# First layer's heads: the two query projections behind the smallest pair of query tiles

## What is computed

```
x = L0_attn_x
xn = _layernorm(x, axis=-1)
x = x + _L0_attn_ref(xn, w_q, w_kv, w_dense) + _L0_ffn_ref(xn, ...)
...
def _L0_attn_ref(x, w_q, w_kv, w_dense):
    q = jnp.einsum('bsh,he->bse', x, w_q).reshape(b, sq, GROUPS, HPG, KVC)
    k, v = jnp.split(jnp.einsum('bsh,he->bse', x, w_kv), 2, axis=-1)
    scores = jnp.einsum('bqgpd,bkgd->bgqpk', q, k) * SCALE
    scores = jnp.where(causal[None, None, :, None, :], scores, -jnp.inf)
    probs = jax.nn.softmax(scores, axis=-1)
    ctx = jnp.einsum('bgqpk,bkgd->bqgpd', probs, v).reshape(b, sq, HEADS * KVC)
    return jnp.einsum('bse,eh->bsh', ctx, w_dense)
```

## Time and profile before

| | us |
|---|---|
| three runs | 3680.51, 3680.76, 3674.75 (median 3680.51) |
| the profiled execution's own time | 3672.85 |
| its span | 3671.1 |
| PE busy in the span | 3376.9 (92%) |
| DVE, ACT, POOL busy | 2423.2, 1566.8, 1182.8 |
| the 16 heads of layer 0, in the span | 75 to 897 |

### The profile page before, as it was taken

The page is one execution under the profiler, slowest core; times in us unless marked ns, Lnnn a source line. Parts: engine busy times, 40 slices in busy tenths (PEclk is TensorE's granted clock), DMA queues, the critical chain, the costliest instruction groups (busy, mean ns, idle before and its releaser), DMA issues. The chain is left out here.

```text
span 3671.1 us, 65160 instructions
## 1 busy us (share of the span) xinstructions
PE 3376.9 (92%) x21360; PEld 2608.3 (71%) x21360; DVE 2423.2 (66%) x4492; ACT 1566.8 (43%) x2872; POOL 1182.8 (32%) x854
## 2 busy tenths in 40 slices
PE   8999999999979999999986779999779998799997
PEld 6888888887758788888862445555358886488883
DVE  4666666666335666566555778886478887488873
ACT  4555555554324444444432236666233333233332
POOL 4011010200236666666643200000124445344444
PEclk9999999999999999999998879999879999899998
DMA  5000000010001000000001412221144442244331
GB/s 176 4 18 11 7 20 3 26 37 1 0 7 50 18 19 13 19 16 19 17 0 53 154 70 81 81 81 61 61 113 113 111 112 68 58 118 110 108 98 49
DMA packets 134113, 199.98 MB, mean 54 GB/s; under 512 B 23120, under 2 KB 78288, under 8 KB 133968
## 3 DMA queue, kind: packets, MB, share of 16 engines
q1 hardware_dynamic: 127888, 190.55, 16.7%
q0 software_dynamic: 6144, 8.39, 1.4%
HBM read 162.06 MB, written 36.57 MB: 54 GB/s over the span
## 5 line engine op out<-in xcount | busy, mean ns | idle before, releaser
L2137 DVE TENSOR_REDUCE l2h_half<-l2h_s 128x1 f32<-128x512 f32 x512 | 337.2, 685 | 48.0 <-PE l2h_s L2039 45.4
L2124 ACT ACTIVATE l2h_PT<-l2h_s 128x1024 f32<-128x1024 f32 x256 | 248.4, 1023 | 163.5 <-PE l2h_s L2049 163.4
L791 DVE TENSOR_REDUCE l0h_negtop<-l0h_sc 128x1 f32<-128x128 f32 (+7 forms) x256 | 192.7, 753 | 161.9 <-PE l0h_sc L687 161.9
L813 DVE TENSOR_TENSOR l0h_PTL<-l0h_tp,l0h_PTH 128x512 fp32r<-128x512 f32 (+3 forms) x384 | 199.9, 549 | 135.3 <-ACT l0h_PTH L869 135.2
L869 ACT ACTIVATE l0h_PTH<-l0h_tp 128x512 fp32r<-128x512 f32 (+3 forms) x384 | 174.6, 490 | 199.5 <-PE l0h_tp L698 197.7
L2039 PE MATMUL l2h_s<-l2h_K,l2h_Q 128*128 128x512 f32 x512 | 219.1, 466 | 22.7 <-DMA l2h_K<-l_split 20.0
L879 ACT ACTIVATE l0h_probs<-l0h_sc,l0h_negtop 128x128 f32<-128x128 f32 (+7 forms) x256 | 191.1, 746 | 90.0 <-DVE l0h_negtop L791 86.3
L159 POOL TENSOR_TENSOR XN<-XN,n_rstd 128x512 f32<-128x512 f32 x24 | 29.9, 1267 | 566.5 <-DVE n_rstd L140 566.5
L765 POOL TENSOR_TENSOR l0a_wq_lo<-l0a_wq,l0a_wq_hi 128x256 fp32r<-128x256 f32 x15 | 11.1, 741 | 591.2 <-ACT l0a_wq_hi L853 591.2
L698 PE MATMUL l0h_tp<-ident,l0h_probs 128*128 128x128 f32 x1152 | 175.6, 277 | 21.4 <-DVE l0h_PTL L813 21.4
L713 PE MATMUL l0h_cx<-l0h_PTH,l0a_VH 128*128 128x256 f32 (+1 forms) x640 | 183.1, 286 | 0.7 <-DVE l0h_PTL L813 0.7
(11 more groups left out here) (449 smaller groups left out, 9903.9 us busy)
## 6 DMA issues: line engine op xcount, KB each, us to landing
l3p_decb<-l_decays SPq DMA_DIRECT2D x128, 256.0 KB, 4.4
l3p_w<-L_w SPq DMA_DIRECT2D x34, 512.0 KB, 3.7
l2h_Q<-l_split SPq DMA_DIRECT2D x64, 256.0 KB
l2h_K<-l_split SPq DMA_DIRECT2D x64, 256.0 KB
l3p_prow<-l_decays SPq DMA_DIRECT2D x128, 128.0 KB, 3.1
l_split<-l2q_hi SPq DMA_DIRECT2D x16, 512.0 KB, 3.6
l_split<-l2q_lo SPq DMA_DIRECT2D x16, 512.0 KB, 3.8
l3p_wgu<-L_ffn_w_gate_up SPq DMA_DIRECT2D x32, 256.0 KB, 4.8
```

Source lines behind the costliest of these rows:

```text
L791: dve.reduce_max(negtop[:, i % 4:i % 4 + 1], sc[s % 2][:, 0:(t + 1) * P], AX_X, negate=True).then_inc(top_ready, 1)
L813: dve.tensor_tensor(PTL[part], tp[n % 2][:, 0:m * P].rearrange("p (m n) -> p m n", m=m), PTH[part].bitcast(F32), ALU.subtract).then_inc(pt ...
L2124: act.activation(PT[:, b, kb, :], s2[kb % 2][:, :], ACT.Exp, scale=L2_SCALE).then_inc(exped, 1)
L2137: dve.reduce_max(half[:, b, t, z:z + 1], bank(slot_of(i))[:, :], AX_X).then_inc(s1_read, 1)
```

## The change

```
-    SLOTS = [("unit", i) for i in range(4)] + [("query", 1)] + [("unit", i) for i in range(4, 12)] + [("query", 0)] + [("unit", i) for i in range(12, 16)]
+    SLOTS = [("unit", i) for i in range(2)] + [("query", 1)] + [("unit", i) for i in range(2, 10)] + [("query", 0)] + [("unit", i) for i in range(10, 16)]
```

## The result

| | before | changed |
|---|---|---|
| median of 7 runs each | 3676.00 | **3659.13** |
| lowest and highest | 3669.98, 3683.11 | 3652.44, 3661.14 |
| profiled execution's own time, its span | 3672.85, 3671.1 | 3659.13, 3657.3 |

The ratio is 0.994, with a 95% interval of 0.9926 to 0.9955: faster by 16 to 27 us. The two medians differ by 16.9. The forecast was 3660, the range 3645 to 3672.

The account below looks back on a forecast made before the run. PE's stream was taken to bound the heads; about 0.6 us won per half over 32 halves, 19 to 20 us, gave 3672.85 - 20 = 3653 for the profiled execution and 3680.5 - 20 = 3660 as median, range 3645 to 3672.

Parts of the forecast that it names:

- The bound: In the 16 heads PE's stream sets the time, 51.4 us per head; only PE's 24.1 us of idle can be won.
- The place of the gain: At a half's start, weighing begins 1.25 us after the first score matmul instead of 1.94, the dense product standing between.
- The chain from tile 7's transposes: At the end of a half, from tile 7's transposes to the second PTL's end: 2.59 us; weighing starts 0.15 later.
- the forecast 50.2: PE's distance from one head to the next falls from 51.4 to about 50.2 us.
- The new wait: Amid tile 6's transposes PE waits 0.35 us for tile 3's PTL, behind tile 7's row maximum on DVE.
- the rest of the half: Up to the next half's start nothing is gained: about 273.0 against 272.93, wait won and wait made nearly cancelling.
- The room for DVE's additions: Moved additions stand ahead of tile 0's row maximum; its probabilities are first needed 6.5 us after the half's start.
- The waits that had to hold: Covers in each half: ctxT with 0.15 us left, POOL's low weights 3.6 us; projection readers finish before tile 3's scores.
- third rival: Dense product behind tile 6's scores waits for ctxT behind tile 3's exponential; at 0.9 us, 10 us slower, 3690; 5%.
- listed under "wrong": Signs of failure: head distance 51 us or more with a tile 6 or ctxT wait, or tile 3's scores awaiting queries' low part.
- The start's clock: At the first head's start, PE at 1.2 GHz: difference put at nothing, at most 2 us.
- The later layers keep their durations: Listed as a sign that the forecast is right: layers after the changed one take as long as before.

Follow-up runs that it names:

- first: Kernel before with its old slots, only the dense product of tiles 2 and 3 and its additions one step later: 3659.02 us against 3680.32, ratio 0.9945.
- third: Changed kernel with only batch 1's projection moved (slot 2), batch 0's left at slot 13: 3664.75 us, one run; 50.40 us per head.
- fourth: Changed kernel with the dense product of tiles 0 and 1 one step later, behind tile 3's transposes: 3644.70 us against 3680.32 before, ratio 0.9907.
- last of the experiments: Changed slots, late dense product of tiles 0 and 1, ACT and DVE doing queries ahead of tile 0's PTH and PTL: 3642.40 us, ratio 0.9904 to before.

## Why the prediction was right, and where its terms were off

**The bound** held. PE's stream sets the heads' time, and what was won is what PE waited.

**The place of the gain** was named rightly: the dense product between tile 7's transposes and tile 0's scores. The first and third experiments show it. The prediction put 0.69 us there (1.94 to 1.25) and the trace has 0.78 (1.94 to 1.16). The chain from tile 7's transposes to the second `PTL`'s end took 2.56 us (243.28 to 245.84), as reckoned (2.59). But the first score matmul came 1.56 us behind the start of those transposes, where 1.5 was put, and the weighing 0.16 behind `PTL`. The distance of the heads fell to 49.6 us, not only to the forecast 50.2.

**The new wait** was named with its place and its cause, and sized 0.35 us; it is 0.25. Together with small differences in the switches, the rest of the half gained 0.02 us instead of losing 0.07. That is the term that was mis-sized: 0.09 at the half's start and 0.09 in the rest make 0.80 instead of 0.62 us per half, 5 to 6 us over 32 halves.

**The room for DVE's additions** was put at 6.5 us from the half's start to the first need of tile 0's probabilities. That left out the projection, which now stands ahead of tile 0's transpose: in the changed kernel it is 8.8 us (244.84 to 253.61). The error was on the safe side.

**The waits that had to hold** did. `ctxT` for tiles 0 and 1 was ready at 235.53 (235.16 + 0.37) and its dense product started at 235.92:

```profile
235.16 0.37 ACT L887 ACTIVATE l0h_ctxT<-l0h_cx 128x256 f32<-128x256 f32 x1
...
235.92 1.03 PE L727 MATMUL l0h_outp<-l0a_wd,l0h_ctxT 128*128 x4
```

0.39 us were left, not 0.15. That the third rival was near is no mere thought: one slot further it made the kernel slower.

**Missed:** the first head. The prediction said that the readers of the projection finish before tile 3's scores need the bank, and priced only the steady heads. In the first half of head 0 no older pair is weighed between the projection and those scores, so the cover of 2.15 us isn't there (timeline of the changed kernel):

```profile
82.33 1.29 DVE L797 SCALAR_TENSOR_TENSOR l0a_QL<-l0h_sc,l0a_QH 128x512 fp32r<-128x512 f32 x2 [0.20 <-ACT l0a_QH L858]
...
83.67 0.50 PE L683 MATMUL l0h_sc<-l0a_KH,l0a_QH 128*128 128x512 f32 x1 [1.36 <-DVE l0a_QL L797]
```

It costs 1.36 us once, and is the wait that the prediction listed under "wrong".

**The start's clock** was put at no difference, and in this pair there is none: over 76 to 80 us the granted clock is 0.57 in both kernels, that is most of it at 1.2 GHz. The changed kernel (the clock is third from the end):

```profile
76.00:80.00 4.00, 3.60 (x13) 2.80 (x12) 0.71 (x2) 1.66 (x5) 3.19 (x1) 0.57 0.77 259
```

PE was a little busier in it (3.60 us instead of 3.45), and the slow stretch was no shorter. By the rule of the Trainium skill (TensorE: Matmul & The Clock Gate, Part 1) that recent activity releases the clock, up to 2 us more were thinkable; this pair shows none of it. But the slow start is not there in every execution. Over the same 4 us the clock is 1.00 in the first, third, fourth and last of the experiments, with PE busy 3.21 to 3.48 us, and 0.56 to 0.63 in the other four, with PE busy 3.45 to 4.00 us. So the higher clock goes neither with one order of the slots nor with a busier PE in these 4 us, and what decides it stays open. It is worth over 1 us: the first projection takes 4.06 us to the next start in the change, and 2.91 in the fourth experiment, whose order is the same there.

**"The later layers keep their durations"** was wrong for this pair of profiles, and why is only known in part. POOL splits the weights of layer 1 in 17 steps, the last 16 of them one per head; first and last start, before and after:

```profile
L1372 POOL TENSOR_TENSOR l1a_w_lo<-l1a_w,l1a_w_hi x17: 1802/1813/1821, 1101.0 to 1876.3; 128x768 fp32r<-128x768 f32 x17
```

```profile
L1372 POOL TENSOR_TENSOR l1a_w_lo<-l1a_w,l1a_w_hi x17: 1800/1814/1820, 1079.6 to 1859.7; 128x768 fp32r<-128x768 f32 x17
```

775.3 us from first to last before, 780.1 after. The change doesn't touch this layer, and the eight experiments, most of which change the first layer's heads as much, have 775.1 to 777.4. That speaks for a property of the execution and not of the change; with one profile of the changed kernel it isn't shown.

With this the profiled pair can be followed from start to end, by how far the changed kernel is ahead of the one before. Where the first layer's second part starts it is 22.9 us (903.76 against 880.89, next section): 22.4 from the 14 distances, less 1.4 up to the first head's split (95.9 to 97.3), where the 1.36 us lie, and 1.8 won behind the last split. At the first split of layer 1 it is 21.4, after the clock's 1.7 (next section); at its last 16.6; at POOL's first split of layer 3 16.9 and at the last 13.7 (its 34 splits took 866.6 us before and 869.8 after, and weren't followed further); at the end 13.8.

**That 3659 came so near to 3660 is partly luck.** The three runs that the forecast started from had a median of 3680.5, and seven have 3676.0. The medians differ by 16.9 us, where 20 was forecast. In the profiled pair the heads won more than that, 22.9 us, and 9 of them were lost again behind the heads by things that the prediction didn't have.

## What to carry to other kernels

In a kernel whose engines walk through one table of slots, moving a big piece moves everything that is counted from it, and the gain may come from a small product that lands in a gap: put only that product there and see, before the big piece is moved. The two aren't independent, though: the big piece's own place was worth 0.21 us per head in one order and 1.24 in another. For each wait that such a gap hides, look for the pair "read of a buffer behind a long reduction on DVE", and compare PE's cover with the chain from the transposes to the end of that read; one slot more or less changed the sign here. Price the first pass by itself, since the work that covers a wait in the steady state may not exist yet.

## What the runs showed of the hardware that was not expected

The clock behind the heads. Between the last head and the first layer's second part PE is idle for 2.92 us in both kernels. In one the clock then stays at 1.00, in the other it falls to 0.50 soon after the matmuls have begun again, and the same ten of 512 columns take 6.25 instead of 4.56 us. The engines by stretch and the timeline, first of the kernel before, then of the changed one (the clock is third from the end):

```profile
904.00:907.00 3.00, 3.00 (x8) 1.33 (x8) 0.43 (x1) 0.69 (x1) 0.00 (x0) 1.00 0.03 5
```

```profile
903.76 4.56 PE L969 MATMUL l0f_bank<-XN,l0r_had 128*128 128x512 f32 x10 [2.92 <-DVE l0f_neg L1061]
```

```profile
882.00:885.00 3.00, 3.00 (x5) 1.21 (x4) 0.41 (x1) 0.69 (x1) 0.00 (x0) 0.50 0.00 0
```

```profile
880.89 6.25 PE L969 MATMUL l0f_bank<-XN,l0r_had 128*128 128x512 f32 x10 [2.92 <-DVE l0f_neg L1061]
```

The idle time is equal to the hundredth, and in the 3 us before its end and the 3 before those PE is busy alike; whether the clock falls was decided by something that these rows don't show. The eight experiments have the same idle 2.92 us. In two of them, the first and the third, the ten matmuls again take 4.56 us; in six they take 6.13 to 7.59, at a clock that fell already within the idle time in five. So one profile can be up to 3.0 us longer than another here, whatever the order in the heads.

Layer 1's heads. With the same instructions the distance from one head of that layer to the next is either 49.2 to 49.4 us or 50.4 to 50.6. Of the last 14 distances 3 were long in the profile before and 7 in the one after; the eight experiments have 3 six times, 4 and 5. Four more long ones make the 4.8 us above. What picks one or the other wasn't found. This bounds how finely a single profiled pair can be compared by its span, and is why the distance between the heads of the touched layer was the better measure here.
